# Routed experts: the signal on which expert weights are asked for, and one row copy made two

## The reference

```python
# layer 0: 16 experts 512 -> 256 -> 512, gelu, the best 4 of a node, 2 shared experts
probs = softmax(x @ gate_w.T); top_v, top_i = top_k(probs, 4); w = softmax(top_v)
out = sum_e w[:, e] * (gelu(x @ w1[e] + b1[e]) @ w2[e] + b2[e]) + shared / 2
# layer 1: 16 experts 512 -> 2 x 384 -> 512, a gated unit, the best 2 of a node, 1 shared expert
out = sum_e w[:, e] * (swiglu(x @ w1[e] + b1[e]) @ w2[e] + b2[e]) + shared
```

## Time and profile before

| | |
|---|---|
| median of 3 runs | 2367.56 us (2363.34 to 2369.09) |
| the profiled execution | 2370.24 us, its span 2368.2 us |
| TensorE busy | 2173.5 us, 92% of the span, 7344 instructions |
| VectorE, ScalarE, GpSimd busy | 1003.9 (42%), 508.1 (21%), 286.6 us (12%) |
| routed stage of layer 0 | first scatter at 843.07 us, last at 1099.8, 48 tiles |
| routed stage of layer 1 | first scatter at 2127.42 us, last at 2357.5, 28 tiles |
| weights of one expert, layer 0 | 512 + 128 KB up and bias, 512 KB down |
| weights of one expert, layer 1 | 1536 + 384 KB up and bias, 768 KB down |

### The profile page before, as it was taken

One profiled execution on the slowest core, in us unless ns is written; L12 is line 12 of the kernel. 1 busy time (PEld: TensorE's weight loads), 2 busy tenths in 40 slices (PEclk: granted clock), 3 DMA queues, 4 the chain that ended last, 5 costly groups with the idle time before them and its releaser, 6 DMA issues. The chain is left out here.

```text
span 2368.2 us, 26639 instructions
## 1 busy us (share of the span) xinstructions
PE 2173.5 (92%) x7344; PEld 1249.5 (53%) x7345; DVE 1003.9 (42%) x2731; ACT 508.1 (21%) x903; POOL 286.6 (12%) x317
## 2 busy tenths in 40 slices
PE   6998889999998988884999989999999999989997
PEld 3444444445455454442544468864478854535554
DVE  7966778302015522112124465511255413725543
ACT  2112221110103022222210144311153212201111
POOL 1200000000000044443210000000000010013333
PEclk9999999999999999997999999999989999999998
DMA  4003000000003257677200000010000001248774
GB/s 125 1 0 117 1 1 18 1 18 0 0 1 126 67 130 175 148 171 165 67 1 4 23 36 1 1 62 0 8 28 1 1 5 57 84 156 243 234 238 97
DMA packets 77201, 154.57 MB, mean 65 GB/s; under 512 B 10217, under 2 KB 21524, under 8 KB 77116
## 3 DMA queue, kind: packets, MB, share of 16 engines
q1 hardware_dynamic: 59452, 113.06, 14.5%
q0 software_dynamic: 17664, 40.43, 8.6%
HBM read 119.50 MB, written 36.18 MB: 66 GB/s over the span
## 5 line engine op out<-in xcount | busy, mean ns | idle before, releaser
L1933 PE MATMUL bank<-arena 125*125 125x257 f32 x1600 | 355.8, 383 | 4.7 <-DVE arena L1852 4.7
L1933 PEld LDWEIGHTS bank<-arena 125*125 125x125 f32 x1600 | 302.2, 189 | 60.5 <-DVE arena L1852 6.3
L2182 PE MATMUL bank<-arena 128*128 x832 | 260.3, 448 | 12.4 <-issue 6.6
L990 PE MATMUL bank<-arena 125*128 125x500 f32 (+1 forms) x720 | 253.5, 513 | 3.1 <-ACT arena L1019 2.3
L481 PE MATMUL bank<-arena 128*125 128x512 f32 x480 | 212.6, 592 | 2.1 <-ACT arena L558 1.0
L2182 PEld LDWEIGHTS bank<-arena 128*128 128x128 f32 x832 | 153.7, 195 | 111.1 <-issue 61.5
L1727 PE MATMUL bank<-arena 128*125 128x512 f32 x480 | 207.8, 592 | 1.0 <-PEq L408 1.0
L990 PEld LDWEIGHTS bank<-arena 125*128 125x128 f32 x720 | 135.5, 189 | 121.1 <-issue 109.7
L2202 PE MATMUL bank<-arena 128*128 x360 | 178.7, 627 | 7.8 <-ACT arena L2259 7.7
L2307 DVE TENSOR_TENSOR arena<-bank,arena 128x384 f32<-128x384 f32 (+1 forms) x104 | 51.6, 497 | 264.6 <-PE bank L2182 248.5
L1911 ACT ACTIVATE arena<-arena 125x625 f32<-125x625 f32 x160 | 134.5, 900 | 102.4 <-DVE arena L1852 102.2
(11 more groups left out here) (332 smaller groups left out, 2259.7 us busy)
## 6 DMA issues: line engine op xcount, KB each, us to landing
arena<-in_L_ffn_expert_w SPq DMA_DIRECT2D x16, 1536.0 KB
arena<-in_L_ffn_re_w SPq DMA_DIRECT2D x32, 512.0 KB
arena<-in_L_ffn_expert_w SPq DMA_DIRECT2D x16, 768.0 KB
arena<-in_L_mix_Wqkv SPq DMA_DIRECT2D x6, 1024.0 KB, 16.3
arena<-in_L_gnn_W SPq DMA_DIRECT2D x3, 2048.0 KB, 8.4
arena<-in_L_ffn_expert_b SPq DMA_DIRECT2D x16, 384.0 KB
token_rows<-arena SPq DMA_DIRECT2D x2, 2500.0 KB
arena<-in_L_gnn_W SPq DMA_DIRECT2D x3, 1024.0 KB, 5.5
```

The lines of the kernel that those rows point to most:

```text
L990: last = pe.matmul(st.bank[4 + n % 4][:, 0:cn], h[s][:, f * P:(f + 1) * P], st.counts[:, s, c0:c0 + cn], start=(s == 0), stop=(s == NT - 1))
L1933: return pe.matmul(st.bank[n % OUTS][0:TS, 0:ONCOL], prob[:, u % 2, s, j * TS:(j + 1) * TS], st.slots[:, head + 1, s, :], start=(s == 0), ...
L2182: last = pe.matmul(st.bank[UP[b][h]][:, 0:WP], xt[b][:, k, :], rt.ring[:, bass.ds(r, 1), k * W + h * WP:k * W + (h + 1) * WP].rearrange("p ...
```

## The change

SP waits for expert e's slot on `add_begun` in place of `down_ready`, against the same number. `down_ready` reaches it when the last down product of expert e - 3 is done; `add_begun`, which begins at zero, when the scatter of the first tile of expert e - 2 begins. The pair `own_row` becomes `get_row` and `add_row`, with a copy and a semaphore each. The number to add to is still copied before tile g's gather; the one to gather by is copied a turn earlier, between the gather and the scatter of tile g - 1, behind a wait for the gather last made from that register's buffer. The last tile makes no copy for a next gather. `weigh` is unchanged, and `row_copied` now counts the copies of the numbers to add to.

```diff
-    own_row = [ar.take(2).bitcast(I32) for _ in range(2)]
+    get_row, add_row = ([ar.take(1).bitcast(I32) for _ in range(2)] for _ in range(2))
...
                 if e >= R:
-                    sp.wait_ge(down_ready, sp.value_load(rt.done_by[0:1, e - R:e - R + 1], min_val=1, max_val=TILES + 1))
+
+                    sp.wait_ge(add_begun, sp.value_load(rt.done_by[0:1, e - R:e - R + 1], min_val=1, max_val=TILES + 1))
                 load_expert(sp, rt, kind, ins, e)
...
-            def know_row(b, pair):
-                pool.tensor_copy(own_row[b], pair).then_inc(row_copied, 1)
+            def know_get(g, b):
+
+                pool.tensor_copy(get_row[b], rt.row_of[:, bass.ds(g + AHEAD, 1), 1:2].rearrange("p a w -> p (a w)")
+                                 ).then_inc(get_copied, 1)
+
+            def know_add(g, b):
+                pool.tensor_copy(add_row[b], rt.row_of[:, bass.ds(g + AHEAD, 1), 0:1].rearrange("p a w -> p (a w)")
+                                 ).then_inc(row_copied, 1)
 
             def gather(g, b):
 
                 pool.wait_ge(rows_used, g + 3)
-                pool.wait_ge(row_copied, g + 2)
+                pool.wait_ge(get_copied, g + 1)
...
             def add_rows(g, b):
+                pool.wait_ge(row_copied, g + 2)
                 pool.wait_ge(y_made, g + 3)
...
-            def tile(i, g, b):
+            def tile(i, g, b, last=False):
...
-                pool.wait_ge(rows_loaded[b], i * 16 + (48 - 16 * b))
                 pool.wait_ge(landed[b], i * 16 + (16 - 16 * b))
-                know_row(b, rt.row_of[:, bass.ds(g + AHEAD, 1), :].rearrange("p a w -> p (a w)"))
+                know_add(g, b)
                 gather(g, b)
+                if not last:
+
+                    pool.wait_ge(rows_loaded[1 - b], i * 16 + 48)
+                    know_get(g + 1, 1 - b)
                 for odd in range(2):
                     pool.wait_ge(landed[odd], earlier[odd])
                 add_rows(g, b)
...
             pool.wait_ge(rt.sums_set, 16 * NT)
+            know_get(0, 0)
             for g in range(2):
-                know_row(g, rt.row_of[:, g + AHEAD, :])
+                know_add(g, g)
+                pool.wait_ge(rows_loaded[g], 32)
                 gather(g, g)
+                if g:
+                    pool.wait_ge(rows_loaded[0], 48)
+                know_get(g + 1, 1 - g)
```

More of the change, by code:

```diff
@@ L2063, in stage_routed @@
         row_copied, all_added, first_copied = sem("row_copied"), sem("all_added"), sem("first_copied")
+        get_copied = sem("get_copied")
         add_begun, gather_begun = sem("add_begun"), sem("gather_begun")
@@ L2108, in gather @@
                     out=rows[b], out_offset=None, in_=rt.table,
-                    in_offset=bass.IndirectOffsetOnAxis(ap=own_row[b][:, 1:2].bitcast(mybir.dt.uint32), axis=0)
+                    in_offset=bass.IndirectOffsetOnAxis(ap=get_row[b].bitcast(mybir.dt.uint32), axis=0)
                     ).then_inc(rows_loaded[b], 16)
             def add_rows(g, b):
+                pool.wait_ge(row_copied, g + 2)
                 pool.wait_ge(y_made, g + 3)
@@ L2115, in add_rows @@
                 pool.indirect_dma_start(
-                    out=sums, out_offset=bass.IndirectOffsetOnAxis(ap=own_row[b][:, 0:1].bitcast(mybir.dt.uint32), axis=0),
+                    out=sums, out_offset=bass.IndirectOffsetOnAxis(ap=add_row[b].bitcast(mybir.dt.uint32), axis=0),
                     in_=y[b], in_offset=None, compute_op=ALU.add, **bounds).then_inc(landed[b], 16)
-            def tile(i, g, b):
+            def tile(i, g, b, last=False):
                 earlier = [pool.value_load(rt.landed_by[odd][0:1, bass.ds(g, 1)], min_val=16, max_val=16 * TILES)
                            for odd in range(2)]
-                pool.wait_ge(rows_loaded[b], i * 16 + (48 - 16 * b))
                 pool.wait_ge(landed[b], i * 16 + (16 - 16 * b))
-                know_row(b, rt.row_of[:, bass.ds(g + AHEAD, 1), :].rearrange("p a w -> p (a w)"))
+                know_add(g, b)
                 gather(g, b)
+                if not last:
+                    pool.wait_ge(rows_loaded[1 - b], i * 16 + 48)
+                    know_get(g + 1, 1 - b)
                 for odd in range(2):
@@ L2153, in _ @@
                     tile(i, i * 2 + (2 - b), b)
-            tile(more, more * 2 + 1, 1)
+            tile(more, more * 2 + 1, 1, last=True)
             for b in range(2):
```

## The result

The changed kernel takes 2399.39 us in the median (2397.03 to 2402.69), the kernel before 2368.22 (2363.34 to 2369.09), four runs each: ratio 1.0137, interval 1.0118 to 1.0156. It is 31 us slower. Its profiled execution has a span of 2398.6 us against 2368.2.

The account below looks back on a forecast made before the run. Layer 0 was taken as bound by a loop through POOL's waits for scatters to land, layer 1 by TensorE without a gap. +32 + 8 - 8 = +32 on 2370.24, less 2.7 for the median, gave 2400 us; 8-in-10 range 2374 to 2421.

Parts of the forecast that it names:

- The new wait in tiles: Layer 1: each expert's first tile, read from SP's asks, compared with the first tile of expert e - 2.
- layer 1's sum: Layer 1: up products wait for late expert weights, 34.2 us less 1.9 of today's waits, +32 us.
- seven stalls: Layer 1 up products: two waits of 11.2 us, four of 2.7, and expert 4's of 1.
- Expert 14's (2.7): Layer 1: expert 14's first tile, 24, three tiles after its gate's, 21, so its up product stalls 2.7 us.
- the signs that I had named: Layer 1: two waits of 10 to 12 us, four or five of 2 to 4; asks within 0.5 us of a scatter.
- The clock: Layer 1's TensorE: its clock falls after stalls, costing +8 us, from 0 to 13.
- Layer 0: Layer 0's scatter loop: cycle falls from 17.45 us to between 16.0 and 17.1 for nine experts, -8 us.
- split copies: POOL's row copies in both layers: separate, earlier copying changes nothing, 0, with bounds of -4 and +4 us.
- rivals 2: Layer 0 reaches the load-free pace, -20 us; layer 1 +24 with no clock loss: 2372, no change; chance 0.14.
- rival 3: Layer 0 cycle 14.2 us, -29; layer 1's loads take 7 us, +18; net -11: 2357; chance 0.07.
- 4: SP's gate does nothing since each load waits for the one before anyway: 2368 us; chance 0.03.
- 5: Both layers lose: layer 0 +10 us from slow first scatters, layer 1 +36 +13: 2427; chance 0.08.

Follow-up runs that it names:

- e6: Changed kernel with add_begun beginning at one, so SP asks at the scatter of expert e - 3's own last tile, in both layers: 2391.59 us.
- e9: Changed kernel with the old signal, down_ready, for two of layer 1's loads, experts 5 and 13: 2371.42 us.
- e5: Changed kernel, but in layer 1 SP waits for the down product of the next expert's first tile in place of its scatter: 2385.51 us.
- e2: Changed kernel with the old signal, down_ready, in both layers, so the split copies alone: 2365.27 us, ratio 0.9995.
- e1: Kernel before with the new signal alone, add_begun in both layers, the row pair copied as one: 2398.91 us.
- e8: Kernel before with layer 0's weight loads of experts 3 to 15 replaced by three transfers of 16 rows of 256 bytes: 2337.15 us.
- e7: Changed kernel with layer 1 on the old signal and SP asking in layer 0 at the scatter of expert e - 2's second tile: 2371.57 us.
- e11: Kernel before, row pair copied as one, with SP asking in layer 0 at the scatter of expert e - 2's second tile: 2371.82 us.

## Why the prediction was right

The total, 2400 against 2399.39, is closer than the working deserves: errors inside the sum cancelled, and that part is luck.

**The new wait in tiles, and layer 1's sum.** Right in mechanism and size: +40 predicted, 40.8 measured, and e6 and e9 show both halves of it (the tile's delay, and each expert by its own gate). I counted seven stalls and 34.2 us; there were five and 34.6. Expert 4's (1 us) did not come, since expert 3's stall had put off its need by more (in e5, where that stall is shorter, it does come, 1.95 us). Expert 14's (2.7) cannot come, because I had read its first tile as 24 from a count of two tiles an expert: tile 24's up product begins at 2346.15 without a wait, 7.2 us after expert 14's ask (2338.91), while no wait of TensorE's here ended sooner than 9.0 us after its ask (e6), so tile 24 must still be expert 13's. The reference's routing gives expert 13 four tiles, 22 to 25, and expert 14 only tile 26. Nothing in the rows before fixed the tiles behind 22, and I should have said so. The rest made it up: short stalls were 3.7 to 4.0 us and not 2.7, for the five loads took 9.9 to 11.5 us from ask to TensorE and not 9.2, and the ask came 1.26 us behind the product and not 2.0 (I had read the scatter's start for the signal's). Why the loads are slower is open: they start beside a scatter and a gather, but so they do in e6, where experts 5 and 13 took 9.0 and 10.0. Two of the signs that I had named came out otherwise for the same reasons: there are three short waits and not four or five, and the asks stand 0.7 to 0.8 us ahead of their scatters in the rows above and not within 0.5.

**The clock.** +8 predicted, 9.0 measured, but evenly: all five restarts lost 1.6 to 2.1 us, where I had given the long ones 2.5 and half of the short ones nothing. No run shows the 2.5: behind the waits of 12.07 and 11.12 us the eight matmuls took 2.1 and 1.7 us more than undisturbed. Nor does one show the upper end of 13, seven stalls at the 1.8 us of the earlier trace rows. In the kernel before the granted clock was 0.50 over 6 us, in a wait of 3.06 us and the work behind it. All five waits of the changed kernel, of 3.67 us and more, cost clock (0.58 to 0.64 over the restarts); shorter waits went either way here, see below.

**Layer 0.** The loop was right leg by leg: 8.2 + 2.3 + 5.5 predicted for the shorter cycle, 7.9 + 2.3 + 5.5 measured. I took the middle of -13 and -3; the medians say -8 to -9, the profiled pair -12.9. For the split copies "0, with bounds of -4 and +4" holds: e2 is at 0.9995, and e1 and the changed kernel are alike. What failed is a bound: that layer 0 could gain at most 20 to 29 us by TensorE's pace. e8 gained 40 in the stage. The forecast did not rest on it, but rivals 2 and 3 were priced by it, and rival 3 was thereby worth less than it could have been; it didn't come since the expert's first scatter, with the load asked just ahead of it, took 7.9 us to land, where rival 3 needed less than 6.4.

**Scatters beside a load.** A scatter took longer to land with a load just asked for than without, 7.9 us against 5.5, but not every scatter by the same: with no other scatter in flight, at an expert's first, it took 7.9 us, with an earlier scatter and a gather just issued, at the second or last, 10.1 and 10.4. That what else is in flight makes the difference is read from this comparison; no run changes it alone.

**Rivals.** 2 and 3 failed on layer 1's loads, which took longer, not shorter. 4 and 5 did not show: layer 0 got faster, and experts 5 and 13 pay the full delay.

## What to carry to other kernels

When a ring slot's reload is tied to a later signal, write down for each group in the ring how many work items lie between that signal and the first use; the groups with the fewest items pay, and an average (1.75 tiles an expert here) hides them. Two signals that differ by one item in code can be best in different stages: choose each where the next group's slack is known. And a transfer that others wait for fared best beside a big load, here, where it was the only scatter in flight (7.9 us to land, against 10.1 and 10.4).

## What I had not expected of the hardware

- A 128-row accumulating scatter lands within 5.5 us when no load has just been asked for (changed kernel, 957.07 to 962.61), and in 5.8 to 5.9 with a load of 1.15 MB asked 1.3 us *behind* it (kernel before, four waits like the one at 940.67). With that load asked 0.74 us ahead of it and no other scatter in flight it takes 7.9, and 10.1 (e7, and e11 with the load asked 1.1 us ahead) or 10.4 us (e6) with an earlier scatter just ahead of it. Layer 0's loads cost 35 us by the medians (31.5, and the 3.3 by which e8's layer 1 is longer) or 40 by the stage of the profiled runs, though the DMA share is 0.70 in the kernel before.
- The length of a wait alone does not say whether TensorE's clock falls. In e9 eight matmuls after 3.29 us took 2.84 us, at a granted clock of 1.00, and after 3.60 us 4.48, at 0.62; in e5 they took 4.11 (0.67) after only 1.95 us and 2.84 (1.00) after 1.76; in e1 5.48 (0.50) after 3.34 us. TensorE's timeline of e9:

```profile
2149.45 4.48 PE L2199 MATMUL bank<-arena 128*128 x8 [3.60 <-DMA arena<-in_L_ffn_expert_b]
...
2288.93 2.84 PE L2199 MATMUL bank<-arena 128*128 x8 [3.29 <-DMA arena<-in_L_ffn_expert_b]
```

- In the changed kernel TensorE does nothing from 2171.24 until 2183.31, tile 8's wait. The granted clock is 0.84 in the mean from 2171 to 2175, then stands at 0.50 until 2187, 3.7 us into the work behind the wait; the next 4 us are at 0.95 (columns as in rows 1):

```profile
2171.00:2175.00 4.00, 0.24 (x1) 0.00 (x0) 1.71 (x4) 1.19 (x2) 3.10 (x4) 0.84 0.53 125
2175.00:2179.00 4.00, 0.00 (x0) 0.00 (x0) 0.00 (x0) 0.00 (x0) 0.13 (x1) 0.50 1.03 372
...
2183.00:2187.00 4.00, 3.69 (x6) 2.18 (x7) 0.00 (x0) 0.00 (x0) 0.00 (x0) 0.50 0.03 11
2187.00:2191.00 4.00, 4.00 (x15) 2.28 (x15) 0.56 (x1) 0.48 (x1) 0.00 (x0) 0.95 0.00 0
```
